# Attention and expert kernel on one core: mean and variance steps of the softmax-and-norm stage moved between VectorE and GpSimd, router choices read from PSUM

## The reference, cut to what matters

```python
# layer 1: attention weights, added to x
kv  = ctx @ W_k.T + b_k                      # per batch: 512 x 128
out = layernorm(x) @ kv                      # 512 x 128
sim = out @ kv.T * scale                     # 512 x 512
sim = (sim - mean) * rsqrt(var + 1e-6) * gamma + beta
x   = x + softmax(sim)
# layer 2: top 2 of 8 experts, on the normed rows
n      = (x - mean(x)) / sqrt(var(x) + 1e-5)
scores = n @ Wg.T                            # 8 scores a row
w      = softmax(top_2(scores))
x      = x + sum_e w_e * (silu(n @ W1[e].T) * (n @ W2[e].T)) @ W3[e].T
```

## Time and profile before

| what | value |
|---|---|
| median of 3 runs | 405.08 us (404.69 to 406.89) |
| span of the profiled execution | 403.3 us (first to last instruction; the profile gives no other time for it) |
| instructions | 8243 |
| PE busy | 359.9 us, 89% |
| DVE busy | 272.8 us, 68% |
| ACT busy | 265.2 us, 66% |
| POOL busy | 160.6 us, 40% |
| mean granted clock of TensorE | 0.938 |

### The profile page before, as it was taken

The page is one execution under the profiler, slowest core; times in us unless marked ns, Lnnn a source line. Parts: engine busy times, 40 slices in busy tenths (PEclk is TensorE's granted clock), DMA queues, the critical chain, the costliest instruction groups (busy, mean ns, idle before and its releaser), DMA issues.

```text
span 403.3 us, 8243 instructions
## 1 busy us (share of the span) xinstructions
PE 359.9 (89%) x2301; PEld 237.5 (59%) x2301; DVE 272.8 (68%) x709; ACT 265.2 (66%) x457; POOL 160.6 (40%) x189
## 2 busy tenths in 40 slices
PE   6876988989787678899999999999999999999981
PEld 5553656756585444555666666666666666666650
DVE  1253574979968889999667676676766767667660
ACT  1277686778866697897656666566665666656650
POOL 2124453454740503464543424435244352443422
PEclk9999989899855599999999999999999999999997
DMA  7998789986950212235435354353453645535333
GB/s 231 420 413 336 259 275 339 399 280 228 277 183 2 79 28 54 54 55 101 82 81 105 60 101 79 79 103 67 96 81 80 103 62 98 81 80 101 67 45 52
DMA packets 21834, 57.61 MB, mean 143 GB/s; under 512 B 4832, under 2 KB 4960, under 8 KB 20256
## 3 DMA queue, kind: packets, MB, share of 16 engines
q0 software_dynamic: 8736, 20.53, 28.4%
q1 hardware_dynamic: 11040, 21.62, 15.0%
q10 hardware_dynamic: 2016, 14.94, 10.3%
HBM read 38.17 MB, written 18.91 MB: 142 GB/s over the span
## 4 chain that ended last, share of the span: by engine, by line
PE 56%; DVE 9%; issue 4%; ACT 3%; DMA 2%; POOL 1%; POOLq 0%; ACTq 0%; DVEq 0%
PE bank L1208 32%; PE bank L1242 16%; PE bank L1199 4%; PE bank L1228 3%; DVE Wp L794 2%; DMA out<-kvj_s,sidx 1%; DVE stage L941 1%; ACT stage L620 1%; DMA ng_s<-n_table,gidx 1%; PE bank L1116 1%; DVE x_s L973 1%; DVE kvg_s L947 1%; PE bank L1100 1%; PE bank L1043 0%; DVE stage L820 0%
## 5 line engine op out<-in xcount | busy, mean ns | idle before, releaser
L941 DVE SCALAR_TENSOR_TENSOR stage<-W,w3sc,stage 128x512 f16<-128x512 f16 x117 | 84.1, 747 | 7.5 <-ACT stage L620 7.5
L1242 PE MATMUL bank<-stage,n_s 128*128 128x512 f16 (+1 forms) x351 | 82.2, 379 | 2.8 <-issue 1.5
L1208 PE MATMUL bank<-Wp,kvg_s 128*128 x480 | 79.9, 317 | 4.6 <-DVE kvg_s L947 4.6
L620 ACT ACTIVATE stage<-W,w3sc 128x512 f16 x117 | 80.1, 717 | 0.0
L1208 PE MATMUL bank<-Wp,kv_s 128*128 x456 | 74.3, 313 | 3.2 <-DVE kv_s L947 3.2
L1208 PEld LDWEIGHTS bank<-Wp,kvg_s 128*128 128x128 f16 x480 | 47.3, 99 | 31.5 <-issue 6.1
L469 POOL DMA_INDIRECT out<-oT_s,sidx x20 | 34.2, 1708 | 75.8 <-ACT oT_s L647 65.0
L1208 PEld LDWEIGHTS bank<-Wp,kv_s 128*128 128x128 f16 x456 | 44.4, 98 | 28.1 <-issue 4.5
L965 DVE TENSOR_TENSOR n_s<-bank,n_s 128x384 f16<-128x384 f32 x39 | 21.7, 556 | 55.1 <-ACT n_s L633 55.1
L469 POOL DMA_INDIRECT out<-kvj_s,sidx x19 | 32.5, 1711 | 66.1 <-ACT kvj_s L647 63.6
L1242 PEld LDWEIGHTS bank<-stage,n_s 128*128 128x128 f16 (+1 forms) x351 | 34.2, 98 | 36.1 <-issue 3.3
(11 more groups left out here) (187 smaller groups left out, 532.3 us busy)
## 6 DMA issues: line engine op xcount, KB each, us to landing
Wp<-in_w ACTq DMA_DIRECT2D x6, 1408.0 KB, 9.0
W<-in_w ACTq DMA_DIRECT2D x8, 768.0 KB, 5.7
stage<-in_xT SPq DMA_DIRECT2D x4, 1024.0 KB, 7.8
W<-in_x SPq DMA_DIRECT2D x12, 256.0 KB, 7.3
out<-W SPq DMA_DIRECT2D x12, 256.0 KB, 6.5
Wp<-in_w SPq DMA_DIRECT2D x2, 1408.0 KB, 12.7
n_table<-n_s SPq DMA_DIRECT2D x8, 256.0 KB, 3.2
n_table<-x_s SPq DMA_DIRECT2D x8, 256.0 KB, 3.3
```

Source lines behind the costliest of these rows:

```text
L620: eng.activation(w3p[t % 2][:, c * D:(c + 1) * D], W3[:, bass.ds(e * W3N + c * D, D)], ACT.Copy, scale=w3sc[:, bass.ds(e, 1)]).then_inc(s_ ...
L941: eng.scalar_tensor_tensor(w3p[r][:, W3N + c * D:W3N + (c + 1) * D], W3[:, bass.ds(e * W3N + c * D, D)], w3sc[:, bass.ds(e, 1)], w3p[r][:, ...
L1208: mm = eng.matmul(bank[2 * which + r][:, 0:H], n_, w_, start=(c == 0 and k == 0), stop=(c == DC - 1 and k == 2))
L1242: mm = eng.matmul(ybank(t - 1)[:, :], h_, w_, start=(c == 0 and k == 0), stop=(c == HC - 1 and k == 2))
```

## The change

The row sum of x1 is no longer accumulated. `xneg` is formed on POOL, ahead of `alpha`, as -mean(x) - 1/512, from `mv`, which is there a slot or more earlier. `va` moves from DVE to POOL as well. `xneg` gets four columns in place of two. The copy of the scores goes away; the maximum and the places are read from the scores in PSUM, and what waited for the copy waits for the places.

```diff
             def scale(b, i):
                 g, k = g_of(b, i), i % 2
+                eng.wait_ge(s_mv, g + 1)
+                wait(eng, s_sq, g - 3)
+                wait(eng, s_n, g - 3)
+                eng.tensor_scalar(xneg[:, g % 4:g % 4 + 1], mv[:, k, 0:1], -1.0, -1.0 / D, ALU.mult, ALU.add).then_inc(s_xn, 1)
+                eng.wait_ge(s_msq, b + 1)
+                eng.tensor_scalar(va[:, k:k + 1], mv[:, k, 1:2], N * SEPS, msq[:, i:i + 1], ALU.mult, ALU.add).then_inc(s_va, 1)
                 eng.wait_ge(s_va, g + 1)
                 wait(eng, s_T, g - 1)
                 eng.tensor_tensor(alpha[:, k:k + 1], va[:, k:k + 1], half[:, :], ALU.pow).then_inc(s_al, 1)
...
-                eng.tensor_scalar(n_t[g % 4], x_s[g], xneg[:, k:k + 1], rstd[:, k:k + 1], ALU.add, ALU.mult).then_inc(s_n, 1)
+                eng.tensor_scalar(n_t[g % 4], x_s[g], xneg[:, g % 4:g % 4 + 1], rstd[:, k:k + 1], ALU.add, ALU.mult).then_inc(s_n, 1)
...
                     eng.wait_ge(s_xn, g + 1)
+                    eng.wait_ge(s_x1, g + 1)
...
             def mean_square(b):
                 eng.wait_ge(s_mp, b + 1)
+                wait(eng, s_va, TPB * b)
...
                 eng.bn_stats(bn[:, k, :], x_s[g]).then_inc(s_bn, 1)
-                hold(eng, 3, (s_bn, g + 1))
+                eng.wait_ge(s_bn, g + 1)
+                wait(eng, s_va, g - 1)
                 eng.bn_aggr(mv[:, k, :], bn[:, k, :]).then_inc(s_mv, 1)
-
-            def scale_in(b, i):
-                g, k = g_of(b, i), i % 2
-                eng.wait_ge(s_mv, g + 1)
-                eng.wait_ge(s_msq, b + 1)
-                wait(eng, s_al, g - 1)
-                eng.tensor_scalar(va[:, k:k + 1], mv[:, k, 1:2], N * SEPS, msq[:, i:i + 1], ALU.mult, ALU.add).then_inc(s_va, 1)
...
-                    eng.scalar_tensor_tensor(x_s[g], L_s[:, k, :], einv[:, k:k + 1], x_s[g], ALU.mult, ALU.add,
-                                             accum_out=xsum[:, k:k + 1]).then_inc(s_x1, 1)
-                    eng.wait_ge(s_x1, g + 1)
-                    eng.tensor_scalar(xneg[:, k:k + 1], xsum[:, k:k + 1], -1.0 / D, None, ALU.mult).then_inc(s_xn, 1)
+                    eng.scalar_tensor_tensor(x_s[g], L_s[:, k, :], einv[:, k:k + 1], x_s[g], ALU.mult, ALU.add).then_inc(s_x1, 1)
...
-                    eng.tensor_copy(sc[:, :], score_bank(g)[:, 0:E]).then_inc(s_sc, 1)
-                    hold(eng, 5, (s_sc, g + 2))
-                    eng.max(top[:, i3, :], sc[:, :]).then_inc(s_top, 1)
-                    hold(eng, 6, (s_top, g + 1))
-                    eng.max_index(topi[:, i3, :], top[:, i3, :], sc[:, :]).then_inc(s_ti, 1)
+                    eng.max(top[:, i3, :], score_bank(g)[:, 0:E]).then_inc(s_top, 1)
+                    eng.wait_ge(s_top, g + 1)
+                    eng.max_index(topi[:, i3, :], top[:, i3, :], score_bank(g)[:, 0:E]).then_inc(s_ti, 1)
...
             def weight_norms(n):
-                wait(eng, s_sc, n - 4)
+                wait(eng, s_ti, n - 4)
...
                 if score_bank(g) is bank[7]:
-                    eng.wait_ge(s_sc, g + 1)
+                    eng.wait_ge(s_ti, g + 1)
```

More of the change, by code:

```diff
@@ L151, in build @@
         einv = sb("einv", [P, 2])
-        xsum = sb("xsum", [P, 2])
-        xneg = sb("xneg", [P, 2])
+        xneg = sb("xneg", [P, 4])
         ssq = sb("ssq", [P, 2])
@@ L157, in build @@
         rstd = sb("rstd", [P, 2])
-        sc = sb("sc", [P, E])
         top = sb("top", [P, TPB, 8])
@@ L533, in slot @@
                     eng.wait_ge(s_xn, g + 1)
+                    eng.wait_ge(s_x1, g + 1)
                     wait(eng, s_vd, g - 1)
                     wait(eng, s_sq, g)
-                    eng.activation(junk[:, :], x_s[g], ACT.Square, bias=xneg[:, k:k + 1],
+                    eng.activation(junk[:, :], x_s[g], ACT.Square, bias=xneg[:, g % 4:g % 4 + 1],
                                    accum_out=ssq[:, k:k + 1]).then_inc(s_sq, 1)
@@ L802, in slot @@
                     x_stats(bn_, in_)
-                    if i < TPB - 1:
-                        scale_in(bn_, in_)
                 if real(b):
@@ L867, in _ @@
             eng.memset(spare_v[:, 13:14], 0.0).then_inc(s_scp, 1)
-            eng.memset(spare_v[:, 14:15], 0.0).then_inc(s_sc, 1)
             eng.memset(spare_v[:, 15:16], 0.0).then_inc(s_ti, 1)
```

## The result

The changed kernel takes 412.4 us (median of 4 runs, 412.04 to 415.05) where the kernel before takes 405.64 us in the same comparison: ratio 1.0171, 95% interval 1.0138 to 1.0205. It is slower by 6.8 us; the forecast was 406.3 us, with a range from 403.2 to 408.9.

The account below looks back on a forecast made before the run. The attention stage up to the first gather was taken as bound by POOL's loop through alpha and ACT's evacuation and square. Terms 2.76 - 0.60 - 0.46 - 0.75 - 0.20 + 0.50 = +1.25 us on 405.08 gave 406.3 us, range 403.2 to 408.9.

Parts of the forecast that it names:

- p = 0.46 us: POOL between n and alpha: the two added small instructions and a wait delay alpha by 0.46 us a tile.
- L503's start 0.08 after alpha: Sign of being right: ACT's scaled evacuation of tiles 3, 6, 7 and 11 starts 0.08 us after alpha.
- 0.20 for the copy: End of the attention stage: DVE loses one copy of the scores, -0.20 us.
- the routers' later release: Routers on PE wait for max_index instead of the copy, 0.28 us later; costed at nothing, +0.8 without cover.
- Collisions: Batch 0's columns on DVE can delay alpha of tile 11 by 0 to 1.4 us; taken as +0.5.
- The six alpha-bound steps: Tiles 3, 6, 7, 11, 13 and 14, where the evacuation waits for alpha: 6 x 0.46 = +2.76 us.
- My rival of held-up POOL: Wide DVE instructions hold up POOL's additions: +2.0 on six tiles, +0.9 at the columns, 408.7 us; chance 0.20.
- tiles 5, 9 and 10, -0.46: DVE reaches its minimum 0.2 to 0.4 us earlier, POOL's added work takes half back: together -0.46 us.
- tiles 4, 8 and 12, -0.60: Accumulator read and xneg leave DVE's queue ahead of msq, so alpha comes earlier: -0.2 us each, -0.60.
- the clock's case of my rivals: PE's matmul clock changes: -3.0 us, 403.3; the other way, a batch's gram product doubles, +1 each; chance 0.09.
- theory 3: Experiments' third explanation of the loss: the matmul clock; for the PSUM part, no more than 1 us either way.
- tile 15, -0.75: Last tile's exp and evacuation: DVE's relief takes back part of the +1.70 us delay, leaving +0.95: -0.75.

Follow-up runs that it names:

- The swapped kernels: On POOL, alpha of the last tile of batches 0 to 2 ahead of the gamma product: on the kernel before 402.25 us, on the changed kernel 405.72 us.
- the PSUM run: Kernel before, with the maximum and the places read from PSUM and the copy of the scores gone: 406.16 us, ratio 1.0007.
- two dummies: Kernel before, with two more 128x1 instructions on constants on POOL ahead of each alpha, which waits for both: 414.5 us, ratio 1.0247.
- the three edits of the changed kernel that keep both on POOL: Changed kernel with batch 0's columns waiting for tile 11's alpha, 411.07 us; last tiles' pairs ahead of the preceding norm, 407.33; alpha swapped before gamma product, 405.72.
- the run with the waiting columns: Changed kernel, with DVE's columns of batch 0 waiting until alpha of tile 11 is done: 411.07 us, ratio 1.0108.
- the one with pairs moved into the idle time: Changed kernel, with both small POOL instructions of each batch's last tile ahead of the preceding norm, where POOL waits for ACT's square: 407.33 us, ratio 1.0038.
- the swap on the changed one: Changed kernel, with alpha of the last tile of batches 0 to 2 and its two small instructions ahead of POOL's gamma product: 405.72 us, ratio 0.9988.
- All 32 memsets: Kernel before, with two 128x1 memsets on POOL ahead of each alpha, which waits for both: 407.72 us, ratio 1.0047.

## Why the prediction was wrong

**Right: the place.** POOL's stretch between n and alpha is what the change lengthens, and the loop through ACT's square passes it on. Taking the two instructions off POOL ends the loss, adding their like to the kernel before makes one as large.

**Right: the plain price.** I took p = 0.46 us. Where nothing disturbs it the steps grew by 0.52, 0.51 and 0.53 (to norm 1, 4 and 5): xneg 0.19, va, which reads a second input, 0.26, and the wait. The swapped kernels differ by 0.51 in the same steps (5.43 and 4.92). Of the signs that I had named, L503's start 0.08 after alpha came true; DVE's busy time fell by 8.2 us and not by 9 to 10.

**Right: what passes unchanged.** PE's stretch is 7.70 us and fully busy; the step from norm 15 to the gather became 0.23 us shorter where I had 0.20 for the copy; the tile loop kept its length. At nothing I had costed the routers' later release, and the PSUM run agrees.

**Wrong: the term "Collisions", +0.5.** This is the step that failed. I looked for them at one tile, and asked which instruction of DVE meets alpha there in the schedule of before. The six alpha-bound steps grew by 6.24 us in all, against 2.76 + 0.50. The plain price at the measured 0.52 makes 3.1, so what hold-ups added is 3.1 us: 1.1 in the step to norm 9 (the experiment's 1.3 at the columns of batch 0, less the 0.18 that the kernel before paid there), and by difference 0.57 in the step to norm 11 and 1.42 in the step to norm 12. At those two I had expected none. The durations give the same: in the step to norm 11 `vd` and `rstd` lasted 0.54 and 0.33 us longer than undisturbed, where the kernel before lost 0.32 at `vr`; in the step to norm 12 `vr`, n and xneg lasted 0.53, 1.02 and 0.42 longer, where the kernel before lost 0.56. So most of it fell on instructions that both kernels have, and not on the two that came.

```profile
98.12 0.73 POOL L412 TENSOR_TENSOR vd<-ssq,inv_d 128x1 f32<-128x1 f32 x1 [1.55 <-ACT junk L541]
...
99.20 0.88 POOL L417 TENSOR_TENSOR rstd<-vr,half 128x1 f32<-128x1 f32 x1
...
103.84 0.72 POOL L414 TENSOR_TENSOR vr<-vd,eps_x 128x1 f32<-128x1 f32 x1
```

The timeline shows the largest, of the wide n itself:

```profile
105.29 1.79 POOL L420 TENSOR_SCALAR x_s<-W,xneg,rstd 128x512 f32<-128x512 f32 x1
105.31 0.69 DVE L751 TENSOR_TENSOR stage<-steps,rf 128x1024 f16<-128x1024 f16 x1
...
105.93 0.68 DVE L753 TENSOR_TENSOR stage<-steps,qf 128x1024 f16<-128x1024 f16 x1
...
106.53 1.09 DVE L755 TENSOR_TENSOR stage<-stage,tok 128x1024 f16<-128x1024 f16 x1
107.06 0.61 POOL L401 TENSOR_SCALAR xneg<-mv 128x1 f32<-128x1 f32 x1
```

Before, n of tile 11 was done at 100.87 and the same columns came from 102.39 on, beside two small steps that lost 0.5 us. Later POOL and earlier DVE have come together: the change itself made the meeting. The other runs fit this, though none was made for it. With POOL later and DVE as before (two dummies) the step to norm 12 is 5.16 us, with both instructions back on DVE it is 4.50, and in the three edits of the changed kernel that keep both on POOL it is 6.73 to 6.75.

My rival of held-up POOL, with a chance of 0.20, had the mechanism, and its 2.0 + 0.9 us for the hold-ups are near the 3.1. That is luck in part: it spread the 2.0 over six tiles by the mean of L410, while the steps to norm 1, 4 and 5 had none, and two others had all of it. With p and the hold-ups at their measured size the sum would have been +4.2 us; the other 1.9 come from the terms that follow. (With the other terms as they stand, the forecast's own range adds up to 404.9 to 408.1 and not 405.0 to 407.9, which changes nothing here.)

**Wrong: tiles 5, 9 and 10, -0.46.** I gave half of DVE's relief back; all of it went, and more: +0.20, +0.16 and +0.31 in the steps to norm 3, 7 and 8. Tile 9 shows how, POOL after DVE's mean and variance:

```profile
74.54 0.59 POOL L401 TENSOR_SCALAR xneg<-mv 128x1 f32<-128x1 f32 x1 [1.57 <-DVE mv L697]
75.11 0.26 POOL L403 TENSOR_SCALAR va<-mv,msq 128x1 f32<-128x1 f32 x1
75.46 0.91 POOL L406 TENSOR_TENSOR alpha<-va,half 128x1 f32<-128x1 f32 x1
```

Here xneg falls beside DVE's minimum and alpha beside its x1. ACT's evacuation starts 0.08 after alpha's end, at 76.45. It was held by the exp before (alpha's end at 74.52, the start at 75.11); it is held by alpha now. Tile 5 is another case: its evacuation still follows the exp without a wait, and it is DVE's minimum that starts later, 0.35 us after the instruction ahead of it, for a reason that the profile doesn't show.

**Partly wrong: tiles 4, 8 and 12, -0.60.** Two gave -0.14 each (I had -0.20). The third is +0.40: the gram product ahead of it ran at 1.92 us instead of 1.10. That is the clock's case of my rivals, "the other way", with about the +1 that I named: where the same product took 1.10 us, in the run with the waiting columns, the step is 6.13 us in place of 6.95. It is the only large place before the table where the clock costs the changed kernel more than the one before; the first product is at its slow length in both. So theory 3 explains about 0.8 of 6.1 us in the traced execution. That the change brought it about is not shown: the same product took 2.04 us after 1.78 us of idle time with only `xneg` on POOL, and 1.37 after 3.42 with two dummies.

**Too large: tile 15, -0.75.** It was -0.48 in its step, and -0.37 by norm 15.

**The 6.13 us by cause:** plain length 3.1; hold-ups in the six steps 3.1; tiles 5, 9 and 10 +0.7; the clock at one product about +0.8; the gains -1.6: batch starts about -0.7 without the clock, tile 15 and behind it -0.37, end -0.23, and the start -0.30, which is of the size of chance. The first three I put down to DVE's relief by the terms of the prediction; no run shows it for each. Of the rest of the span's 6.7 us, 0.6 lies behind the gather and is of the size of the spread between runs.

## What to carry to other kernels

An engine that is busy for 40% of the time can still be the one that sets the pace, in the stretch between what it is given and what it hands on. Ask where in its order a moved instruction stands, not how much idle time it has: the same two instructions made the ratio 1.0171 behind n and 1.0038 when four of the sixteen pairs stood in POOL's wait (a third of that gain was the clock's). And moving one long instruction from in front of the awaited one to behind it was worth 3.9 us, while relieving the busier engine of the copy and the accumulator was worth nothing that could be measured. Last, when an instruction moves, look for new meetings over the whole schedule as it will be, of all instructions of both engines, and not at one tile of the schedule as it was.

## What the hardware showed that I had not expected

**A small POOL instruction can be passed by two wide DVE instructions in a row.** In the changed kernel va, at 86.94, lasted 1.24 us and ended 0.05 after the second of them; the dummy with two inputs took 1.23 us in the same situation:

```profile
88.76 0.68 DVE L759 TENSOR_TENSOR stage<-steps,qf 128x1024 f16<-128x1024 f16 x1
88.86 1.23 POOL L404 TENSOR_SCALAR pdum<-half,inv_d 128x1 f32<-128x1 f32 x1
89.36 0.68 DVE L761 TENSOR_TENSOR stage<-stage,tok 128x1024 f16<-128x1024 f16 x1
```

The one-input instruction just before it (0.65 us, at 88.24) was held by one DVE instruction only. In the four kernels in which both of the pair ran beside the columns (the changed one, two dummies, the one with pairs moved into the idle time, the swap on the changed one) it was always the one with two inputs that was held twice, 1.22 to 1.24 us. It was also always the later of the pair. Which of the two is the reason no run here separates.

**What doesn't read isn't held.** All 32 memsets took 92 to 103 ns, the ten inside a wide two-input DVE instruction too. The Trainium skill ("SBUF — State Buffer", two separate sides) says that a DVE instruction with two SBUF inputs shuts out a GpSimd one only if that one reads SBUF; the runs agree. The same section of the Trainium skill says that the first comer keeps the ports for its whole instruction. L755, which grew to 1.09 us beside n, fits that. But n's record starts 0.02 us ahead of L751's, and it was n that grew, to 1.79 us, and not L751 (0.69); and va shows that a waiting POOL instruction needn't be next. In these rows the order of the recorded starts doesn't tell who is held.

**Reading 8 values from PSUM costs DVE nothing here.** The maximum takes 170 ns from either memory, the places 166 against 160 ns (before, then after):

```profile
L847 DVE MAX8 top<-sc 128x8 f32<-128x8 f32 x16 | 2.7, 170 | 0.7 <-DVE sc L845 0.2
L849 DVE FIND_INDEX8 topi<-top,sc 128x8 uint32<-128x8 f32 x16 | 2.6, 160 | 0.0
...
L838 DVE MAX8 top<-bank 128x8 f32<-128x8 f32 x16 | 2.7, 170 | 8.8 <-PE bank L1106 8.7
...
L840 DVE FIND_INDEX8 topi<-top,bank 128x8 uint32<-128x8 f32 x16 | 2.6, 166 | 0.0
```

The 62 cycles more that the Trainium skill ("VectorE: DVE Perf Modes", the TRN2 errata) gives for a PSUM source are not in these rows.
